# A vision-tower kernel on one Trainium2 core: the leaves of four more decision trees are fetched by indirect DMA instead of computed densely

## What is computed

```python
h = patchify(x, 16) @ tok_W.T + tok_b                       # 64 x 196 x 256
# attention on y = layernorm(h)
xn = y / max(norm(y) / 16, 1e-5) * g
u, v, base = split(silu(xn @ uv_w.T))                       # 512, 512, 128
q, k = rope(base * gamma + beta)
kernel = square(relu((q @ k.T + w_rel[...]) / sqrt(128)))
h = h + y * res_scale + (u * (kernel @ v)) @ o_w.T
# 8 trees of depth 7, 255 nodes each, on z = layernorm(h)
logits = z @ W_in.T + b_in                                  # 8 x 255 per token
acts = silu(logits)
current = 0
for d in range(7):                                          # walk down each tree
    current = child(current, logits[current] > 0)
h = h + (acts * visited) @ W_out.T                          # 8 visited nodes per tree
```

## Time and profile before

| | us |
|---|---|
| median of 3 runs | 2206.93 (2206.41 to 2209.72) |
| the profiled execution, its own time | 2201.36 |
| its span in the trace | 2199.5 |
| PE busy in it | 2066.1 (94%) |
| DVE busy | 1621.5 (74%) |
| ACT busy | 1395.2 (63%) |
| POOL busy | 774.1 (35%) |

### The profile page before, as it was taken

The page is one execution under the profiler, slowest core; times in us unless marked ns, Lnnn a source line. Parts: engine busy times, 40 slices in busy tenths (PEclk is TensorE's granted clock), DMA queues, the critical chain, the costliest instruction groups (busy, mean ns, idle before and its releaser), DMA issues.

```text
span 2199.5 us, 42461 instructions
## 1 busy us (share of the span) xinstructions
PE 2066.1 (94%) x13256; PEld 1941.8 (88%) x13256; DVE 1621.5 (74%) x4210; ACT 1395.2 (63%) x3085; POOL 774.1 (35%) x905
## 2 busy tenths in 40 slices
PE   6899999999999999999999999999999999999997
PEld 5789889899988898888998898988889988889887
DVE  5678777777777787777777777777777877777775
ACT  5556666666666566566666665666665666656654
POOL 2752333232333333332323333323323233333233
PEclk8999999999999999999999999999999999999999
DMA  5331322222322223222223222222223232222222
GB/s 146 85 94 52 89 73 66 73 76 63 83 71 65 81 55 84 75 64 73 77 62 84 70 73 73 64 75 77 65 70 84 55 85 69 73 73 66 63 67 74
DMA packets 81999, 163.13 MB, mean 74 GB/s; under 512 B 17102, under 2 KB 48048, under 8 KB 81968
## 3 DMA queue, kind: packets, MB, share of 16 engines
q0 software_dynamic: 40960, 103.02, 17.4%
q1 hardware_dynamic: 41008, 59.71, 9.3%
HBM read 148.76 MB, written 13.90 MB: 74 GB/s over the span
## 4 chain that ended last, share of the span: by engine, by line
PE 84%; another core or an unknown queue 5%; ACT 4%; POOL 3%; issue 2%; DVE 1%; DMA 1%; ACTq 0%; POOLq 0%; SPq 0%; DVEq 0%
PE front L1142 10%; PE front L1144 9%; PE front L1143 9%; PE hid_ps L1142 9%; PE hid_ps L1143 9%; PE hid_ps L1144 9%; PE out_acc L1142 6%; PE out_acc L1143 6%; PE out_acc L1144 6%; PE out_acc L1378 4%; PE front L1177 2%; PE front L1184 2%; PE hid_ps L1366 2%; PE hid_ps L1337 2%
## 5 line engine op out<-in xcount | busy, mean ns | idle before, releaser
L474 POOL DMA_INDIRECT leaf_rows<-leaf_table,leaf_at x512 | 532.4, 1040 | 163.9 <-issue 163.4
L453 POOL TENSOR_TENSOR inv_root<-to_root,minus_half 98x8 f32<-98x8 f32 x64 | 111.0, 1734 | 728.3 <-DVE to_root L885 404.6
L528 ACT ACTIVATE hid_hi<-hid 128x392 fp32r<-128x392 f32 (+1 forms) x256 | 177.8, 695 | 237.1 <-PE out_acc L1144 155.4
L1142 PE MATMUL out_acc<-hid_hi,outw_lo 128*128 128x392 f32 x768 | 293.4, 382 | 2.6 <-DVE hid_lo L835 2.3
L1142 PE MATMUL hid_ps<-ffn_x,in_lo 128*128 128x392 f32 x768 | 282.3, 368 | 6.2 <-POOL in_lo L445 5.8
L1143 PE MATMUL hid_ps<-ffn_x,in_hi 128*128 128x392 f32 x768 | 266.3, 347 | 0.0
L1144 PE MATMUL hid_ps<-ffn_x,in_hi 128*128 128x392 f32 x768 | 264.7, 345 | 0.0
L1144 PE MATMUL out_acc<-hid_hi,outw_hi 128*128 128x392 f32 x768 | 264.6, 345 | 0.0
L1143 PE MATMUL out_acc<-hid_lo,outw_hi 128*128 128x392 f32 x768 | 264.4, 344 | 0.0
L473 POOL TENSOR_TENSOR held<-minus_half 98x1 f32<-98x1 f32 x128 | 47.2, 369 | 489.9 <-issue 428.7
L718 ACT ACTIVATE leaf_rows<-leaf_rows,leaf_act 98x256 f32<-98x256 f32 x512 | 218.2, 508 | 0.1
(11 more groups left out here) (140 smaller groups left out, 5808.2 us busy)
## 6 DMA issues: line engine op xcount, KB each, us to landing
x_raw<-x SPq DMA_DIRECT2D x192, 196.0 KB, 2.4
out<-out_stage SPq DMA_DIRECT2D x32, 392.0 KB
leaf_rows<-leaf_table,leaf_at POOLq DMA_INDIRECT x512
leaf_table<-leaf_rows SPq DMA_DIRECT2D x4, 256.5 KB, 4.7
out_stage<-in_w SPq DMA_DIRECT2D x4, 256.0 KB
tok_major<-tok_w SPq DMA_DIRECT2D x3, 256.0 KB, 4.3
late_raw<-out_w SPq DMA_DIRECT2D x6, 128.0 KB
u<-uv_w SPq DMA_DIRECT2D x1, 576.0 KB, 4.2
```

What stands on the lines that cost most here:

```text
L453: pool.tensor_tensor(inv_root[:, 0:size], to_root[:, 0:size], minus_half[:, 0:size], ALU.pow).then_inc(roots_ok, 1)
L474: pool.indirect_dma_start(row_slot(s, g), None, table, bass.IndirectOffsetOnAxis(ap=leaf_at[:, s, g:g + 1], axis=0), element_offset=s * P ...
L528: act.activation(out, src, ACT.Copy).then_inc(done, 1)
L1142: pe.matmul(out, w[1], x_parts[0], start=start, stop=False)
```

## The change

GATHERED goes from 4 to 8, so that the leaves of all eight trees are fetched and no tree has a second half. `hid`, `hid_hi` and `hid_lo` keep their size but become a ring of four trees (HID_SLOTS = 4), the fetched rows get 16 slots (four trees), and the lists of calls on PE, ACT, DVE and POOL are written in another order. What the dense leaves needed at the start (a permuted bias column, leaf weights loaded in eight pieces) goes; the table in DRAM has eight trees.

```diff
-GATHERED = 4
+GATHERED = 8
 DENSE = TREES - GATHERED
 PIECES = O_PIECES + GATHERED + 2 * DENSE
 ROW_IN, ROW = D + 1, 2 * D + 1
-ROW_SLOTS = 8
+HID_SLOTS, HID_HALVES = 4, 1
+ROW_SLOTS = 16
...
-LATE_SPLITS = (((0, 1), (2,), (3,), (4,), (5,)), ((6,), (7,), (8, 9), (10, 11), (12, 13)))
+LATE_SPLITS = (((0, 1), (2,), (3,), (4,), (5,)), ((6,), (7,), (8,), (9,), ()))
...
-        hid = sb("hid", [P, 2 * 2 * T], F32)
-        hid_hi = sb("hid_hi", [P, 2, 2, T], F32R)
-        hid_lo = sb("hid_lo", [P, 2, 2, T], F32R)
+        hid = sb("hid", [P, HID_SLOTS * HID_HALVES * T], F32)
+        hid_hi = sb("hid_hi", [P, HID_SLOTS, HID_HALVES, T], F32R)
+        hid_lo = sb("hid_lo", [P, HID_SLOTS, HID_HALVES, T], F32R)
...
                 else:
                     act.wait_ge(decided, TREES * i + t + 1)
-                if b == halves(t) - 1 and (t >= 2 or not first(i)):
-                    act.wait_ge(hid_lo_ok, TREES * i + t - 1)
+                if b == halves(t) - 1 and (t >= HID_SLOTS or not first(i)):
+                    act.wait_ge(hid_lo_ok, TREES * i + t - HID_SLOTS + 1)
...
             def hid_high(i, t):
...
-                if t >= 2 or not first(i):
-                    act.wait_ge(tree_added, 2 * (TREES * i + t - 1))
-                high(hid_hi[:, t % 2, 0:halves(t)], hid_t[:, t % 2, 0:halves(t)], hid_hi_ok)
+                if t >= HID_SLOTS or not first(i):
+                    act.wait_ge(tree_added, 2 * (TREES * i + t - HID_SLOTS + 1))
+                high(hid_hi[:, t % HID_SLOTS, 0:halves(t)], hid_t[:, t % HID_SLOTS, 0:halves(t)], hid_hi_ok)
...
                 fetch_rows(i, 3, 3)
+                fetch_rows(i, 4, 0)
...
+                fetch_rows(i, 7, 3)
                 norm_roots(n, 1)
                 norm_roots(nx, 0)
...
-                leaf_dots(i, 3)
-                x_low(nx, 3)
...
+                leaf_dots(i, 7)
                 x_low(nx, 5)
...
                 turn_h(n, 0, 0)
                 turn_h(n, 0, 1)
+                add_rows(p, 6)
                 tree_logits(i, 0, 0)
...
+                tree_logits(i, 1, 0)
+                add_rows(p, 7)
...
```

More of the change, by code:

```diff
@@ L408, in _ @@
             load_late(range(O_PIECES))
-            for row, leaf, step, rows in LEAF_RUNS:
-                src = cols[leaf:leaf + step * (rows - 1) + 1:step, COL_B_IN:COL_B_IN + 2 * TREES]
-                sp.dma_start(leaf_col[row:row + rows], src).then_inc(tables_in, 16)
             load_x(1, range(XRING))
@@ L1070, in body @@
                 leaf_dots(i, 0)
-                mask(i, 3)
+                mask(i, 4)
+                if first(n):
+                    build_toward()
+                hid_low(i, 1)
                 rotate_qk(n, 1)
-                hid_low(i, 2)
                 rotate_qk(n, 0)
+                decisions(i, 5)
                 v_low(n, 0)
                 v_low(n, 1)
+                leaf_dots(i, 1)
                 qk_low(n, 0)
+                decisions(i, 6)
                 qk_low(n, 1)
-                leaf_dots(i, 1)
@@ L1080, in body @@
-                if first(n):
-                    build_toward()
-                hid_low(i, 3)
+                hid_low(i, 2)
                 v_low(n, 2)
-                mask(i, 4)
+                v_low(n, 3)
                 add_rel_bias(n, 0)
+                mask(i, 5)
                 square_relu(n, 0)
                 add_rel_bias(n, 1)
-                v_low(n, 3)
+                x_low(nx, 0)
                 square_relu(n, 1)
+                mask(i, 6)
                 kern_low(n, 0)
@@ L1091, in body @@
                 kern_low(n, 1)
-                decisions(i, 5)
-                decisions(i, 6)
-                hid_low(i, 4)
+                leaf_dots(i, 2)
+                leaf_dots(i, 3)
                 gate(n, 0)
-                leaf_dots(i, 2)
                 gate(n, 1)
+                decisions(i, 7)
+                hid_low(i, 3)
                 mix_low(n, 0)
+                x_low(nx, 1)
+                mask(i, 7)
+                x_low(nx, 2)
                 gate(n, 2)
+                gate(n, 3)
@@ L1417, in body @@
                 project_o(i, 1, range(0, EC))
[L1418 removed]
+                embed(n, 1)
+                tree_out(p, 3, 0)
                 turn_h(i, 1, 0)
                 turn_h(i, 1, 1)
[L1421 to L1424 removed]
                 embed(n, 2)
                 embed(n, 3)
+                add_rows(p, 4)
+                add_rows(p, 5)
+                tree_out(p, 3, 1)
@@ L1469, in body @@
-                find_leaf(i, 3)
-                make_v(n, 2)
-                tree_out(i, 2, 0)
-                make_v(n, 3)
-                add_rows(i, 0)
-                tree_out(i, 2, 1)
             body(None, None, None, 0)
```

237 lines of the change are left out of this document (128 added, 109 removed).

## The result

The changed kernel takes 2372.46 us (median; 2369.28 to 2376.75) against 2206.67 before. The ratio is 1.0757, with a 95% interval of 1.0725 to 1.0789: slower by 7.6%, where 4.3% less was forecast. The profiled execution took 2374.85 us, 2373.0 of them its span.

The account below looks back on a forecast made before the run. POOL's loop of eight trees (47.2 us) plus a window (16.2) was taken to bound the kernel at 63.4 us a period, above PE's 61.8. Head 81.9, 31 periods and tail 44.8 + 11.8 gave 2111 us, range 2050 to 2180.

Parts of the forecast that it names:

- The other costs I set at nothing: Slot waits, x loads and the doubled fetches' DMA traffic were given no cost; late landings counted only in POOL's window.
- PE's work: PE's work per period falls from 64.0 to 58.6 us: 48 matmuls go, four `add_rows` and four `find_leaf` come.
- With today's 3.2 us of idle: PE's idle per period, kept unchanged; with 58.6 us of work PE alone would give a period of 61.8 us.
- POOL, eight trees in 47.2: POOL's time for one unit's eight trees of fetches, at 5.9 us a tree.
- rival 3: POOL's preparation slowed by DVE: 6.6 us a tree, period 69.0 us, time 2293 us, slower than before; chance 0.05.
- The window: POOL's stretch from first norm root to next unit's first fetch: 16.2 us, between 14.2 and today's 18.9.
- The head: Time ahead of the first unit's first row fetch, left at 81.9 us.
- The tail: Time from the last unit's first fetch to the end: 44.8 us for eight trees plus 11.8 behind them.
- The sum: Head 81.9, 31 periods of 63.4 and tail 44.8 + 11.8 make a span of 2103.9 us; 2111 us as time.
- rival 1: PE keeps the pace: POOL's loop is 60.6 us, PE's period 61.8, time 2062 us; chance 0.20.
- The rule on descriptors: Skill calls descriptor generation small, the fixed cost mainly completion latency; the row's 1.04 us of POOL per DMA was preferred.
- Rivals 2 and 4: 2: DVE becomes the bound, period 65.2 us, time 2167 us, chance 0.23. 4: the freed time comes back whole, chance 0.02.

Follow-up runs that it names:

- condition A: Label for the sets of runs in which the kernel before took 2201 to 2208 us; the changed kernel takes 2372.46 there. What differs isn't known.
- condition B: Label for the two sets of runs in which the kernel before took 2063 us; the changed kernel takes 2018.80 there, ratio 0.9789.
- before_hold: Kernel before, with POOL issuing tree 1's fetches only when the next unit's base is made; 2064.72 us, ratio 1.0008, in condition B.
- after_few_again: Changed kernel with each fetch bringing 32 of its 98 rows, run again; 2360.93 us, ratio 1.0665, in condition A.

## Why the prediction was wrong

The step that failed is "The other costs I set at nothing", and with it the base of the sum. I priced a fetch by what it takes of POOL. In A it also holds back PE's signals, which no row of POOL shows. That cost was in the profile of before: its fetches are worth 158 of its 2206 us. The row was even quoted, `DVE hT L899 <- remote: 59.3, 31, 3.8`, and read as DVE waiting for PE's work. The table of waits of before had a larger one, which I passed over, the silu of the base. It is PE's first matmuls behind the turns, and its signal is 2.3 to 3.1 us late in nearly every unit:

```profile
ACT bases L591 <- remote: 115.5, 28, 4.2
```

A wait whose releaser the profile can't name, on one core, is a cost to be explained before a change that doubles what stands around it. Doubling the fetches made it 430 us. So the change brought 272 us (430 less 158) of new stalls and low clock, and took off the 105 us that it is worth without fetches: +167 by this sum, 166 measured.

Not all of this is late signals. Condition B has none, and the same kernels take 144 us less there for before (2207 against 2063) and 354 us less for the changed one (2372 against 2019). So the late signals, with the low clock behind them, grew by 210 us, and against a base without them the change gains 44 us: -44 + 210 is the same 166. The rest of the 430 us, 76 us, is what the fetches cost in B over no fetches at all (2018.80 less 1942.68, if the kernel without fetches takes the same in B, as the one with plain DMAs does), and most of that is the loop of POOL that I had priced.

Point by point:

- **PE's work**, forecast 58.6 us a period: the level was right, partly by luck. In B it is 59.35 (mean of the two stretches), and the period without any fetch is 58.47. In A it reads 66.04, since the clock is low for part of it. My 64.0 for before had such a part too: the kernel before has no trace in B, but `before_hold`, which takes the same time, shows PE at work for all of a period of 62.5 us. So the base was 1.5 too high and the saving of 5.4 too large: without fetches the period falls from 62.2 to 58.5 us, by 3.8. "With today's 3.2 us of idle" was wrong as a constant; in B that idle is gone.

```profile
1151.60:1214.10 62.50, 62.50 (x416) 59.91 (x416) 50.26 (x132) 43.22 (x98) 23.20 (x26) 1.00 0.28 77
```

- **DVE** 54.2: measured 54.12 in B and 54.21 in A. **ACT** under 49.6: 48.14. Both right.
- **POOL, eight trees in 47.2**: 46.3 in B. In A a tree's own cost is the same, (1066.4 + 326.7 + 68.7) / 256 = 5.7 us from POOL's groups; rival 3 (6.6 us a tree) is out. But in A POOL waits for `leaf_at` between trees (267 us in all, 60 in B), because `find_leaf`'s signal is late. So POOL doesn't set the pace there.
- **The window** of 16.2: 14.6 in B, 13.8 in A (1220.07 to 1233.85). My lower end of 14.2 was nearer; the wait for the last product that I added is mostly not there.
- **The head**, left at 81.9: 88.8. Four more trees in the table and the first unit's fetches cost 7 us that I had set at nothing. **The tail** of 56.6: 58.8 in B, 62.6 in A.
- **The sum.** In B 88.8 + 31 x 60.38 + 58.8 = 2019.4, the span of its trace. The forecast's 63.4 was 3.0 us a period too long, and rival 1 (61.8) comes nearest by its number, though POOL's loop and not PE sets the period there, as the forecast had it. That is not a late success: in B the kernel before has 62.5 a period (`before_hold`), so the gain is 44 us and not 96.
- **PE's granted clock** was no term of the sum. PE's work takes 179 us longer in A than without fetches, and the granted clock is low for 473 us. Ahead of both low stretches of the period shown PE had stood idle, 4.81 and 1.84 us.
- **The rule on descriptors.** I set the Trainium skill, DMA: Bandwidth & Descriptors, Anatomy of one DMA, against the row. The plain DMAs here still keep POOL for 562 ns, so the row was the better guide; but neither row nor rule told of what the indirect form does to another engine's signals.
- Rivals 2 and 4 did not occur. None of the four had the time come from PE's signals, and with the slower side at 0.05 the chances were too sure for a profile with 182 us of unnamed waits (115.5 + 59.3 + 7.2).

What stays open: what makes condition A, by which path an indirect DMA holds back PE's updates, and whether the recording of the semaphore updates, of which the traces of A lack so many, has a part in it. No run here reaches that.

## What to carry to other kernels

Read the waits with no named releaser as terms of the sum: compare the semaphore's time with the recorded end of what moves it, and ask what else runs whenever they differ. Before doubling an operation, measure the kernel with that operation left out; here two such runs would have told, in condition A, 158 and 105 us in advance. And measure a candidate in more than one session, since the sign of this change depends on it.

## What was not expected of the hardware

- In condition A, updates that PE makes arrive late, by 5.5 us in the stretch shown and in bunches, while POOL issues indirect DMAs; with none issued, or with plain ones of the same size, 0 of 2600 are late. It goes by the number of DMAs (2326 us with 16 of 513 words, 2361 with 32 of 98 rows, 2214 with half the DMAs) and by how closely they follow (140 late in place of 518 when spaced, and no wait without a named releaser). In condition B it doesn't happen. No unnamed wait is for a signal of ACT or DVE. In the runs with late signals the trace lacks many semaphore updates (17334 recorded in `after_few_again`, 31573 for the same kernel in B).
- Two holes of a few microseconds in a period of 73 leave PE at half its clock for about 15 us of it (473 us over 32 units): its matmuls start 0.33 us apart in place of 0.18. Small matmuls put there brought the low time from 473 to 218 us, but at 206 us of work of their own they gave no time back.
- POOL's element-wise instructions of 98x192 with operands in SBUF slowed DVE's products from 422 to 529 ns on average (719 for those that overlap one) and raised DVE's busy time from 1747 to 1968 us for the same instructions. The Trainium skill, SBUF — State Buffer, SBUF: two separate sides, describes a port pair that DVE and GpSimd share as an exclusive lock; by that rule DVE would be held for the length of such an instruction, and this trace agrees in kind.
